# A two-layer attention and LoRA-FFN kernel: the first FFN group's additions moved to the turn, one load moved, and another last product

## The reference, cut to what matters

```python
h  = cond(x)                       # per-sample 64x64 channel mix from a small MLP
y  = attention(h) + gate * adapter_attention(h)
x  = x + y @ w_proj.T              # "projection": 2048 tokens x 1024 x 1024
c  = conv1d(x, weight, taps=9, groups=4) + (cond @ c_weight.T) + bias
base   = c @ W_base.T + b_base     # "FFN": 2048 tokens x 1024 x 1024
logits = c @ W_router.T            # 8 experts, top 2, softmax
lora   = einsum(c @ A, w, B) * 2   # rank 16 for each expert
out = x + base + lora
```

## Time and the profile before

| | before |
|---|---|
| runs, median (lowest to highest) | 1165.27 us (1162.61 to 1166.54) |
| the profiled execution | 1160.39 us |
| its span, first to last instruction | 1158.6 us |
| TensorE matmul busy | 1141.3 us, 99% |
| VectorE busy | 926.9 us, 80% |
| ScalarE busy | 442.2 us, 38% |
| GpSimd busy | 55.2 us, 5% (16 additions of 50.4 us in all) |
| mean granted TensorE clock | 1.000 |

### The profile page before, as it was taken

How to read it: one execution, slowest core, us unless ns; L and a number is a source line. 1 busy time by engine, 2 the same in 40 slices (tenths; PEclk the granted TensorE clock), 3 DMA queues, 4 the chain that set the end, 5 groups by cost and what they waited for, 6 DMA issues and landing times.

```text
span 1158.6 us, 19585 instructions
## 1 busy us (share of the span) xinstructions
PE 1141.3 (99%) x7595; PEld 964.7 (83%) x7595; DVE 926.9 (80%) x1742; ACT 442.2 (38%) x815; POOL 55.2 (5%) x25
## 2 busy tenths in 40 slices
PE   6999999999999999999999999999999999999998
PEld 5988888888888888888888888878888888888887
DVE  5987877877877887887887789887867777877775
ACT  4444454453453553553653644423222212122110
POOL 1000000000000000000000000010000022221112
PEclk9999999999999999999999999999999999999999
DMA  8414124124124033133042188776457933434312
GB/s 260 136 55 136 30 91 137 29 91 137 29 94 134 29 107 121 29 121 108 28 133 96 28 294 319 297 210 195 162 184 286 367 104 98 110 115 114 96 37 91
DMA packets 99577, 151.63 MB, mean 131 GB/s; under 512 B 7306, under 2 KB 84126, under 8 KB 96798
## 3 DMA queue, kind: packets, MB, share of 16 engines
q1 hardware_dynamic: 98478, 135.70, 36.6%
q10 hardware_dynamic: 1008, 14.68, 3.1%
HBM read 95.82 MB, written 54.54 MB: 130 GB/s over the span
## 4 chain that ended last, share of the span: by engine, by line
PE 96%; DVE 2%; issue 1%; ACT 0%; DMA 0%; DVEq 0%; ACTq 0%
PE psum L929 45%; PE psum L1001 25%; PE psum L1019 5%; PE psum L881 3%; PE psum L912 3%; PE psum L897 2%; PE psum L1053 2%; PE psum L260 2%; PE psum L1035 2%; PE psum L941 2%; PE psum L950 1%; PE psum L890 1%; PE psum L1037 1%; PE psum L906 1%; DVE z L353 1%
## 5 line engine op out<-in xcount | busy, mean ns | idle before, releaser
L929 PE MATMUL psum<-z,w_hi 128*128 128x512 f32 x1536 | 480.9, 394 | 0.0
L929 PEld LDWEIGHTS psum<-z,w_hi 128*128 128x128 f32 x1536 | 282.5, 188 | 55.0
L929 PE MATMUL psum<-z,w_lo 128*128 128x512 f32 x768 | 299.9, 391 | 0.0
L1001 PE MATMUL psum<-f_wform,f_act_hi 128*128 128x512 f32 (+1 forms) x912 | 279.7, 389 | 2.6 <-DVE f_act_lo L1455 1.8
L1001 PEld LDWEIGHTS psum<-f_wform,f_act_hi 128*128 128x128 f32 x912 | 167.9, 188 | 36.4 <-DVE f_act_lo L1455 2.3
L1001 PE MATMUL psum<-f_wform,f_act_lo 128*128 128x512 f32 (+1 forms) x456 | 176.0, 386 | 0.0
L1221 ACT ACTIVATE a_kbd<-a_kr 32x512 f32<-32x512 f32 x128 | 80.7, 630 | 234.2 <-DVE a_kr L1358 233.0
L929 PEld LDWEIGHTS psum<-z,w_lo 128*128 128x128 f32 x768 | 144.2, 188 | 30.8
L1001 PEld LDWEIGHTS psum<-f_wform,f_act_lo 128*128 128x128 f32 x456 | 85.7, 188 | 17.6
L855 POOL TENSOR_TENSOR f_xn<-f_x,_bbase 128x1024 f32<-128x1024 f32 x16 | 50.4, 3152 | 1026.4 <-DVE f_x L1505 696.2
L1191 ACT ACTIVATE f_act_hi<-f_act_sum 128x512 fp32r<-128x512 f32 x64 | 40.3, 632 | 118.0 <-DVE f_act_sum L1449 45.3
(11 more groups left out here) (176 smaller groups left out, 1564.9 us busy)
## 6 DMA issues: line engine op xcount, KB each, us to landing
w_forms<-f_prep_lo SPq DMA_DIRECT2D x16, 896.0 KB, 4.7
f_wform<-w_forms SPq DMA_DIRECT2D x7, 2048.0 KB, 12.9
f_wform<-w_forms ACTq DMA_DIRECT2D x7, 2048.0 KB, 17.3
w_st<-in_wqkvT SPq DMA_DIRECT2D x7, 1536.0 KB, 7.0
w_forms<-f_prep_hi SPq DMA_DIRECT2D x16, 640.0 KB, 5.8
m_x<-in_x SPq DMA_DIRECT2D x16, 512.0 KB, 4.2
y_scratch<-a_ysb SPq DMA_DIRECT2D x32, 256.0 KB, 2.6
f_raw<-y_scratch SPq DMA_DIRECT2D x8, 1024.0 KB, 5.9
```

Of the source, the lines that this page charges most:

```text
L929: mm = pe.matmul(dst, w[:, c, x, :], zs, start=(c == 0 and i == 0), stop=(c == KC - 1 and i == 2))
L1001: mm = pe.matmul((prod_bank[i], bank[0])[part][:, cols], a[:, c, :], wform[i][:, w, c, cols], start=(i < 4 and c == 0 and n == 0), stop=(c ...
```

## The change

1. GpSimd's additions for group 8 no longer use group 0's x1 in SBUF. In the turn group (7), SyncE issues `load_x(8, t)` right behind `put_aside(7, t)`; it waits until that write has landed (`x1_out[t]`), since it overwrites the same SBUF rows. GpSimd waits for that load. The waits of group 1's and group 8's `out_half` on these additions and writes go.
2. `load_y(1)` is issued between weight forms 5 and 6. ScalarE's first two `high` of group 1 go ahead of the last `y_copy`, and VectorE's first lows and sums of group 1 go ahead of group 0's `out11` and `out12`.
3. In the last group product 4 (into bA) is moved to the end, behind product 6, and done in two halves with bank 0; products 3 and 6 are whole. The last two VectorE instructions write 256 columns of one row, and the last stores are of 256 columns.

```diff
@@ load_x
                 if ffn(G):
-                    sp.wait_ge(stored[t], 16 * (G - NJ))
+                    if G == NJ:
+                        sp.wait_ge(x1_out[t], 16 * NJ)
+                    else:
+                        sp.wait_ge(stored[t], 16 * (G - NJ))
                     sp.dma_start(x1[:, t, :], x1_dram[p]).then_inc(x_in[t], 16)
@@ unit_step (sync)
-                    for i in range(4, NPROD):
-                        load_form(i)
+                    load_form(4)
+                    load_form(5)
+                    load_y(1)
+                    load_form(6)
@@ proj_group
-                load_y(G + 1)
+                if G >= 1:
+                    load_y(G + 1)
@@ turn_group
                 put_aside(G, 0)
+                load_x(NJ, 0)
                 put_aside(G, 1)
+                load_x(NJ, 1)
@@ ffn_group and the end of sync
-                store_out(G, 0)
+                if G < 2 * NJ - 1:
+                    store_out(G, 0)
...
-            for part in range(2):
-                cols = slice(HALF // 2 * part, HALF // 2 * (part + 1))
-                sp.wait_ge(row2_set, 2 * NJ + part)
-                sp.dma_start(out[NB - 2:NB].rearrange("b c (s n) -> (b c) s n", s=2)[:, :, cols],
-                             x1[:, 1, :].rearrange("p (s n) -> p s n", s=2)[:, :, cols]).then_inc(stored[1], 16)
+            def store_columns(done, cols):
+                sp.wait_ge(row1_set, 2 * (2 * NJ - 1) + done)
+                sp.dma_start(out[NB - 4:NB - 2, :, cols].rearrange("b c l -> (b c) l"), x1[:, 0, cols]
+                             ).then_inc(stored[0], 16)
+
+            store_columns(1, slice(HALF, L))
+            store_out(2 * NJ - 1, 1)
+            store_columns(2, slice(0, HALF // 2))
+            store_columns(3, slice(HALF // 2, HALF))
@@ add_bias
-                if G == NJ and t == 0:
-                    pool.wait_ge(row1_set, 2)
-                elif G == NJ:
-                    pool.wait_ge(row2_set, 1)
-                elif t == 0:
-                    pool.wait_ge(x_in[0], 16 * G)
+                pool.wait_ge(x_in[t], 16 * (G + 1))
+                if t == 0:
                     pool.wait_ge(row1_set, 2 * G - 1)
                 else:
-                    pool.wait_ge(x_in[1], 16 * G)
                     pool.wait_ge(v2_set, G)
@@ product, and group (tensor)
-                parts = 2 if G == 2 * NJ - 1 and prod_bank[i] is bB else 1
+                halved = G == 2 * NJ - 1 and prod_bank[i] is bA
+                if halved and i == 0:
+                    pe.wait_ge(conv_set, 2 * NP)
+                parts = 2 if halved else 1
...
-                product(G, 4)
+                if G < 2 * NJ - 1:
+                    product(G, 4)
...
                 product(G, 6)
+                if G == 2 * NJ - 1:
+                    product(G, 4)
@@ scalar, after attention
             attend_copies(m)
+            high(1, A11)
+            high(1, A22)
             y_copy(m)
-            next_forms(1)
+            next_forms(1, 2)
@@ out_half (vector)
-                    if G == NJ:
-                        dve.wait_ge(x1_out[t], 16 * NJ)
                     return dve.tensor_tensor(x1[:, t, HALF * half:HALF * (half + 1)], src[:], other, ALU.add)
                 wait(dve, x1_out[t], 16 * G)
-                if G == 1:
-                    dve.wait_ge(xn_set, t + 1)
@@ group 0 (vector)
-                    out11(0)
-                    out12(0)
-                    for f in (A11, A22):
-                        low(1, f)
+                    low(1, A11)
+                    low(1, A22)
                     add_up(1, S1)
                     add_up(1, S2)
+                    out11(0)
                     low(1, S1)
                     low(1, A12)
+                    out12(0)
@@ last group (vector)
-                    out11(G)
                     out12(G)
                     share21(G)
+                    row2(G)
                     for part in range(2):
                         cols = slice(HALF // 2 * part, HALF // 2 * (part + 1))
                         dve.wait_ge(prod, NPROD * G + 7 + part)
-                        dve.wait_ge(u21_set, G + 1)
-                        dve.tensor_tensor(x1[:, 1, :].rearrange("p (s n) -> p s n", s=2)[:, :, cols],
-                                          (bB, bank[0])[part][:, cols].rearrange("p (s n) -> p s n", s=1)
-                                          .broadcast_to([P, 2, HALF // 2]), u2[:, :, cols], ALU.add).then_inc(row2_set, 1)
+                        dve.tensor_tensor(x1[:, 0, cols], (bA, bank[0])[part][:, cols], x_of(G, 0)[:, cols], ALU.add
+                                          ).then_inc(row1_set, 1)
```

More of the change, by code:

```diff
@@ L823, in _ @@
                 ffn_group(G)
-            for part in range(2):
-                cols = slice(HALF // 2 * part, HALF // 2 * (part + 1))
-                sp.wait_ge(row2_set, 2 * NJ + part)
-                sp.dma_start(out[NB - 2:NB].rearrange("b c (s n) -> (b c) s n", s=2)[:, :, cols],
-                             x1[:, 1, :].rearrange("p (s n) -> p s n", s=2)[:, :, cols]).then_inc(stored[1], 16)
+            def store_columns(done, cols):
[6 more added lines that the diff above has]
+            store_columns(3, slice(HALF // 2, HALF))
             sp.wait_ge(y_out, 16 * NG * NU)
-            sp.wait_ge(stored[0], 16 * NJ)
-            sp.wait_ge(stored[1], 16 * (NJ + 1))
+            sp.wait_ge(stored[0], 16 * (NJ + 2))
+            sp.wait_ge(stored[1], 16 * NJ)
         @block.gpsimd
@@ L1003, in product @@
                                            skip_group_check=True)
-                    if part == parts - 1 or i == NPROD - 1:
+                    if part == parts - 1 or i == 4:
                         mm.then_inc(prod, 1)
@@ L1048, in low_rank @@
             def low_rank(G, dst, t, part):
-                dsts = (dst[:, 0:HALF // 2], bank[0][:, HALF // 2:HALF]) if G == 2 * NJ - 1 and dst is bB else (dst[:],)
+                dsts = (dst[:, 0:HALF // 2], bank[0][:, HALF // 2:HALF]) if G == 2 * NJ - 1 and dst is bA else (dst[:],)
                 for n, to in enumerate(dsts):
@@ L1112, in group @@
                     pe.wait_ge(hwT_set, G - NJ + 1)
+                    if G == 2 * NJ - 1:
+                        pe.wait_ge(s1_set, G + 1)
                     low_rank(G, bA, 0, 0)
@@ L1195, in first_share, with next_forms @@
                 wait(act, v2_set, G)
+                if G == 2 * NJ - 1:
+                    act.activation(s1[:, 0:HALF // 2], bA[:, 0:HALF // 2], ACT.Copy)
+                    act.activation(s1[:, HALF // 2:HALF], bank[0][:, HALF // 2:HALF], ACT.Copy).then_inc(s1_set, 1)
+                    return
                 act.activation(s1[:], bA[:], ACT.Copy).then_inc(s1_set, 1)
-            def next_forms(G):
-                for f in form_order(G)[:-1]:
+            def next_forms(G, done=0):
+                for f in form_order(G)[done:-1]:
                     high(G, f)
@@ L1486, in share12 @@
                 dve.wait_ge(v2_set, G + 1)
[L1487 to L1491, removed]
                 dve.tensor_tensor(w12[:], bB[:], w12[:], ALU.add).then_inc(w12_set, 1)
@@ L1524, in row2 @@
             def row2(G):
-                dve.wait_ge(prod, NPROD * G + 7)
+                dve.wait_ge(prod, NPROD * G + (6 if G == 2 * NJ - 1 else 7))
                 dve.wait_ge(u21_set, G + 1)
```

## The result

The changed kernel takes 1177.45 us (median, 1176.25 to 1178.74) beside 1163.94 us for the kernel before (1160.88 to 1166.54; the three executions shown ahead and one more): a ratio of 1.0123, interval 1.0103 to 1.0144, so 13.5 us slower. Its profiled execution took 1176.25 us with a span of 1174.5 us, 15.9 us longer than the span of before.

What follows compares the result with a forecast made beforehand. TensorE, 96% of the chain that ended last and at its upper clock, was taken to bound the kernel. -2.6 + 18.6 + 1.8 + 0 - 0.5 = +17.3 us on the median 1165.27 gave 1182.5 us, range 1172 to 1190.

Steps and rivals of the forecast that it cites:

- The chain at the turn: Group 7 to 8: writes, loads, addition, `u2` and `convolved` in sequence make TensorE's second convolution wait, +18.6 us.
- the second write behind the first load: SyncE's queue at the turn: `put_aside(7, 1)` lands 3 us after `load_x(8, 0)`, at 926; bounds 0 and 7.6.
- the Trainium skill's round-robin rule: Turn's first load: engines alternate between queues by packet, so it lands some 8 us after issue; sum +14.8 us.
- the row: Profile entry for a 64 KB load issued at 890.87 beside the forms: 10.5 us, taken for the turn's first load.
- The clock: Behind the stall in group 8: the first convolution runs partly at half rate, +1.8 us, bounds 0 and 3.6.
- The half: Behind the turn's stall: half of the 3.6 us upper bound for slower clock was taken, +1.8 us.
- the light rival: Turn: loads run beside the forms as if alone; stall 9.6 us, no clock loss, +6.5, 1172 us; chance 0.16.
- The gain in groups 0 and 1: Without GpSimd's additions there, TensorE's two waits, for an `act_lo` and `u2`, go: -2.6 us.
- both waits go with part 1 and part 2 is worth 0: Group 1: part 1 removes TensorE's two waits, -2.6 us; moving `load_y(1)` adds 0, bounds 0 and +1.6.
- Form 6 and y of group 1: Group 1's start: with `load_y(1)` moved, y lands near 745 and form 6 near 750, hidden with 0.5 us to spare.
- The tail: End of the last group: smaller last VectorE instruction and store, -0.5 us, bounds -0.8 and +0.3.
- The sum: Whole kernel: all terms together +17.3 us, giving 1177.7 for the profiled execution and 1182.5 for the median.

Runs made afterwards that it cites:

- Experiment 5: The changed kernel, with ScalarE issuing weight forms 5 and 6 only when both rows of group 8 are back: 1171.29 us, ratio 1.0067.
- experiment 6: Kernel before, each of GpSimd's two additions for group 8 replaced by three memsets (one execution, no time given) or by one memset (1159.48 us, ratio 0.9970).
- part 1 alone: Kernel before with only the change's part 1 (group 8's rows loaded back at the turn), run twice: 1181.52 and 1180.53 us, ratios 1.0150 and 1.0140.
- experiment 3: Kernel before with only the change's part 3 (the last group's new order and smaller last stores): 1162.41 us, ratio 0.9994.
- experiment 4: The changed kernel with both writes of group 7 issued ahead of both loads: 1177.86 us, ratio 1.0119.
- experiments 1 and 6: The two runs of part 1 alone, and the memset runs of experiment 6.
- experiments 2 and 7: Changed kernel with part 1 undone: 1160.34 us; then part 2 on the kernel before, without GpSimd's additions (one memset each): 1159.75 us, and with them: 1162.16 us.

## Why the prediction was right, step by step

- **The chain at the turn** was the right mechanism, and its size came out within 1.4 us: +18.6 us forecast, 17.2 us measured. With 3.3 us added for what had gone faster up to there, the first load landed at 923.7 (forecast 923.0), the second write at 924.8 (926), the second load at 928.3 (929.5), and the second addition ended at 931.2 (932.6). The term that was off is the second write behind the first load, 1.1 us for 3: the last form was over at 923.6 so counted, where I had it at 924.9, and load and write landed right behind it.
- **The weighing of the Trainium skill's round-robin rule** ("DMA: Bandwidth & Descriptors", section "Queues, rings and completion order") against the row (8 us for the first load by my estimate from the rule, 10.5 by the row) went for the row, at 11.0. That is in part luck: the row was of 64 KB, an eighth of the load. Whether the rule is off or only my estimate (one form beside the load; it landed with the last form instead), no run shows. Experiment 5 shows that 7 of these 11.0 us go with forms 5 and 6: 4.1 us without them.
- **The clock**: +1.8 forecast, 2.55 us measured, inside 0 to 3.6. The half was a guess; my view in the light rival, that a wait of 9.6 us spares the clock, is refuted by experiment 5, where one of 9.1 us cost 1.6 us behind it.
- **The gain in groups 0 and 1**: -2.6 forecast, 3.0 us measured in the change as a whole. That the additions are the cause is shown (experiment 6: 3.2 us). But the step "both waits go with part 1 and part 2 is worth 0" is not: the two waits went, but part 1 alone left others of 2.9 and 1.2 us, since y of group 2 is next to be late. I had not asked what would be late next. Part 2 gives this load 1.7 to 2 us of room. By my estimate from these waits that is worth nothing where y lands in 5.7 us and up to 2 us where it takes 8.8. The medians agree, 1.0123 with parts 2 and 3 against 1.0150 and 1.0140 without, but their intervals overlap.
- **Form 6 and y of group 1**: forecast near 750 and 744.5, measured 749.4 and 744.0; hidden.
- **The tail**: -0.5 forecast; 0.8 us gained behind the last matmul, 0.3 to 0.4 us lost ahead of it (experiment 3).
- **The sum**: -3.0 + 17.2 + 2.55 - 0.5 = +16.3 against 15.9 us between the spans and +17.3 forecast. The medians differ by 13.5 us and the forecast was 1182.5 for 1177.45: I had carried the 4.9 us between the profiled execution of before and its median over to the changed kernel, whose profiled execution is only 1.2 us below its median. The profiled execution of the changed kernel started its projections at 28.4 us, as early as any, and by their granted clock of 0.993 its other three did too. No run shows a reason why they did; to carry the distance over, 3.7 us too much, was the largest single error, larger than that of any term.

## What to carry to other kernels

A value that was computed early at a visible small cost may be worth leaving there: before moving its work to a later point, list the transfers that it then depends on and look up what the DMA queues carry at that moment. And when one wait goes, look for the load that is next to be late; a single profile in which it is in time doesn't show that it always is.

## What the runs showed of the hardware

- A 512 KB transfer on SyncE's queue took 11.0 to 16.0 us beside ScalarE's 2048 KB forms, and 3.3 to 5.0 us once these were gone (the changed kernel, experiments 4 and 5); in experiment 4 a load issued while another was under way took 5.5 us.
- The same 1024 KB load of y, at the same place behind the same work, landed 5.7 to 8.8 us after issue in the profiles of experiments 1 and 6, and 5.7 and 7.7 us in those of experiments 2 and 7.
- TensorE's clock fell to 0.50 in a wait of 9.1 us as well as in one of 17.2 us; the convolution behind it took 5.15 and 6.12 instead of 3.57 us. In the wait of 9.1 us the granted clock was still 1.00 over the first part (922 to 925).
- In the first 20 us the same two matmuls (L251) took 1.05 us in some profiles and 2.00 us in others, though the granted clock is recorded as 1.00 in both; the projections then start at 28.4 to 29.0 us in the first and at 31.2 to 34.2 us in the second. In seven of the eight profiles of the second kind the clock was below 1.00 between 28 and 36 us (0.79 in one, 0.57 in six). I don't know what decides between them.
- GpSimd's memsets (2.98 us) left VectorE's two-tensor instructions at 0.7 us; its additions held one up for 2.9 us.
